# Packing routed tokens without padding: 128 two-expert tiles, and 28 one-expert boundary items run ahead of them

## The chip, the cores and the metric

The kernel runs on 1 core of one Trainium2 chip. The metric is the device time of one execution in microseconds (us); lower is better.

## What is computed

16,384 tokens of width 512 are normalised, and go through two branches whose product is added to the input. The first branch is a fixed circulant filter (computed with small matrices here) and a bit-correcting code; the second routes each token to two of eight experts:

```python
x = L0_attn_x                                   # (16, 1024, 512)
xn = _layernorm(x, axis=-1)
s = _L0_attn_ref(xn, W_el, b_el, W_le, b_le)
g = _silu(_L0_ffn_ref(xn, router_w, expert_weights))   # 8 experts of 512 x 512
x = x + s * g
...
probs = jax.nn.softmax(x @ router_w.T, axis=-1)
topk_vals, topk_idx = jax.lax.top_k(probs, 2)
topk_w = topk_vals / (topk_vals.sum(-1, keepdims=True) + 1e-06)
out = ((combined + remap_bias) * weights).sum(axis=0)  # combined: the two chosen experts' outputs
```

## The kernel before

**Stage 1** (R = 8 rounds of U = 4 groups of GT = 4 tiles of 128 tokens) loads all tokens in order, computes routing logits, and finds for each token its pair of experts. There are NQ = 28 unordered pairs. A token's number is scattered by POOL (16 indirect DMAs each round, `scatter`) into a DRAM table, `pair_tokens`, which has a region of rows for each pair. What later stages need of a token (mean, scale, two expert weights, the corrected bits) is stored as a row of 64 words in the DRAM tensor `token_info` (`weigh`, `info_store`).

**Between the stages** DVE works out from the counts of the pairs which row of `pair_tokens` each tile of stage 2 reads and which experts it uses; POOL reads these rows (`tokT`), and they are transposed into `tile_tok`, a column of token numbers for each tile. `tile_exp` holds each tile's two experts.

**Stage 2** runs over NT = 156 tiles of 128 token slots. Each pair's tokens start at a tile of their own, so a pair's last tile is partly empty; 128 tiles' worth of tokens and 27 possible partly empty tiles, rounded up to a multiple of 4, give 156. All 156 are run. Each engine goes through the tiles in an order written out by hand, and waits on semaphores for the others; a step for tile j is:

- POOL: adds the product to the input (`o2`), gathers the input rows and the `token_info` rows for tile j+4 (`gather`, two indirect DMAs), and scatters tile j's output rows (`scatter_out`).
- DVE: combines the two experts' outputs into `z2` (L970), prepares tile j+2 in `split` (sums and differences of halves, L953 to L957, then a high and a low f16 part, `hi2` L960 and `lo2` L962), copies an index for the next gather (L946), and finishes branch one (L981 to L992).
- PE: 12 matmuls of the first expert (L1133 to L1135), then `front` of tile j+1 (a bf16 transpose L1115 and eight f16 transposes L1119), 12 matmuls of the second expert, and 13 matmuls of branch one (L1147 to L1155).
- ACT: scales the first expert's output from PSUM into `t2` (L580), copies the transposes of tile j+1 from PSUM (`hl2` L573, `bT2` L574), computes silu (L586), and copies a part of branch one (L589).

The first 4 tiles and the last 4 are unrolled; those between run in a hardware loop of 4 tiles a pass.

Of the kernel before, what the change touches and what calls it, by code (L numbers as in the profile page):

```python
# [7 lines left out]
F32 = mybir.dt.float32  # L8
F16 = mybir.dt.float16
# [7 lines left out]
P = 128  # L17
# [36 lines left out]

def routing_constants(NE, cap, TB):

    pairs = [(a, b) for a in range(NE) for b in range(a + 1, NE)]
    first, second = np.asarray(pairs).T
    q = np.arange(len(pairs))
    ramp = NE - np.arange(NE)  # L60
    key = NE * (NE - first) + (NE - second)
    region = q * cap
    carry = np.tile(np.arange(TB) > 0, len(pairs))
    tile = np.arange(P)[:, None] + P * np.arange(2)[None, :]
    not_before = -(np.arange(P)[:, None] >= np.arange(P)[None, :]).astype(np.float64)
    same = np.concatenate([ramp, key, first, second, region, region // P, carry])
    return np.concatenate([np.broadcast_to(same, (P, same.size)), tile, not_before], axis=1)


def build(nc, x_in, W_el, b_el, W_le, b_le, router_w, experts, consts, out):  # L70
# [15 lines left out]
    NT = -(-(T + NQ - 1) // U) * U  # L86
# [10 lines left out]
    pair_slots = pair_tokens.rearrange("r (c o) -> (r c) o", o=1)  # L97

    ctx = ExitStack()
    with ctx:  # L100
# [3 lines left out]
        def sem(name):  # L104
# [8 lines left out]
        CW = NE + 5 * NQ + NQ * TB + 2 + P  # L113
# [26 lines left out]
        rsm = sb("rsm", [P, 26, TB])  # L140
# [11 lines left out]
        tq = sb("tq", [P, 3, NQ])  # L152
        tcmp = sb("tcmp", [P, 2, NQ + 1])
        tone = sb("tone", [P, 2, NQ])
        tmul = sb("tmul", [P, 2, NQ])
        tval = sb("tval", [P, 3, 2])
        trow = sb("trow", [P, 2], I32)
        tokT = sb("tokT", [P, 2, P], I32)
        tokTf = sb("tokTf", [P, 2, P])
        tile_tok = sb("tile_tok", [P, 2 * P], I32)  # L160
        tile_exp = sb("tile_exp", [1, 2, 2 * P], I32)
        gidx = sb("gidx", [P, U], I32)
        sidx = sb("sidx", [P, U], I32)
        small = sb("small", [P, 256])
# [11 lines left out]
        key_c, first_c, second_c, region_c, row_c = (cst[:, o + NQ * i:o + NQ * (i + 1)] for i in range(5))  # L176
        o += 5 * NQ
        carry_c = cst[:, o:o + NQ * TB]
        o += NQ * TB
        tile_c = cst[:, o:o + 2]  # L180
        nbefore_c = cst[:, o + 2:o + 2 + P]
# [28 lines left out]
        (m1, m2, mx1, mx2, zs, d2, e2, p1, p2, den, w1, w2, u1, u2, nlow, nhigh, fix, kmax, kmin, isa, isb,  # L210
         wa1, wa2, wb1, wb2, slotf) = (rsm[:, i] for i in range(26))

        oh12, ux12 = rsc[:, 2:4], rsc[:, 6:8]
        p12, w12, u12, isab, wa12 = (rsm[:, i:i + 2] for i in (7, 10, 12, 19, 21))
        far = xT4[:, :, :, :].rearrange("p b c n -> p (b c n)").bitcast(I32)[:, 0:TROWS]
        info_bits = info[:, :, 16:64].bitcast(BF16).rearrange("p t (g c) -> p t g c", g=3)
# [13 lines left out]
        bT2 = arena[0:96, 10 * E:10 * E + P].bitcast(BF16).rearrange("p (s e) -> p s e", s=2)  # L230

# [10 lines left out]
        def sems(names):  # L242
# [28 lines left out]
        rows_ready, rows_loaded, rows_float, rows_turned, exps_mm, tiles_ready = sems(  # L271
            "rows_ready rows_loaded rows_float rows_turned exps_mm tiles_ready")

        ld_x2 = [sem(f"ld_x2_{i}") for i in range(U)]
        stored = [sem(f"stored{i}") for i in range(2)]
        inf_init, gidx_ready, sidx_ready, raw_ready, uv_ready, hi_ready, split_ready = sems(
            "inf_init gidx_ready sidx_ready raw_ready uv_ready hi_ready split_ready")
        uvT_done, hl_ready, e_done, t_ready, z_ready, g_ready, y_done, y_copied, s_ready, sg_ready, o_ready = sems(
# [14 lines left out]
        def rounds(eng, count, step, head=1):  # L293
# [4 lines left out]
            with eng.Fori(head, count - 1) as i:  # L298
                for k in range(U):
                    step(i, k)  # L300
            for k in range(U):
                step(count - 1, k, last=True)

        def at(i, k, ahead):
            return i + (k + ahead) // U, (k + ahead) % U

# [878 lines left out]
```

## Time and profile before

| | |
|---|---|
| median of 3 runs | 1487.29 us (1484.12 to 1487.79) |
| span of the profiled execution, core 0 | 1491.6 us |
| PE busy | 1306.4 us, 88% |
| DVE busy | 1068.7 us, 72% |
| POOL busy | 888.9 us, 60% |
| ACT busy | 625.0 us, 42% |
| stage 1 and the preparation of stage 2 | from 0 to about 401 us |
| stage 2 | from about 401 us to the end |

The profile lists for one execution what each engine ran and when. The profiler gives no time of its own for this execution beside the span, which is 4.3 us over the median of the three timed runs. A group's idle time is the time for which its engine stood still just ahead of it. PE is TensorE's matmuls, PEld its weight loads.

### The profile page before, as it was taken

To read this page: it belongs to the slowest core of one execution; us is meant where nothing else is said; L and a number is where in the kernel's file an instruction comes from. 1 tells how busy PE (TensorE), PEld (TensorE's weight loads), DVE (VectorE), ACT (ScalarE), POOL (GpSimd) and SP (SyncE) were. 2 spreads that over 40 slices of the span, in tenths; PEclk is the share of its full clock that TensorE was granted. 3 is DMA by queue.
4 is the path that set the end of the run, shared out by engine and by line. 5 is a ranking of instruction groups with operands and counts; after the bars stand their busy time and mean duration, and the time that the engine had idled before them with its cause. 6 is when DMAs were issued, how large, how long until landed. Compare 5 with 4: busy or idle time off the path is not lost. (4 is left out here: it accounts for less than half of the span.)

```text
span 1491.6 us, 30014 instructions
## 1 busy us (share of the span) xinstructions
PE 1306.4 (88%) x8142; PEld 745.6 (50%) x8143; DVE 1068.7 (72%) x3072; ACT 625.0 (42%) x1051; POOL 888.9 (60%) x804
## 2 busy tenths in 40 slices
PE   3966776660299999999999999999999999999996
PEld 2544444330155555555555555555555555555553
DVE  7398777777177777777777777777777777777774
ACT  4654444441144444444444444444444444444442
POOL 1056565566456666666666666666666666666663
PEclk9988888785599999999999999999999999999998
DMA  9664656401112222222222212222222222222000
GB/s 348 229 211 141 155 155 155 127 15 28 36 60 84 68 73 75 74 65 72 74 71 73 79 62 71 73 74 77 67 75 62 76 69 71 77 79 63 18 0 1
DMA packets 77222, 129.97 MB, mean 87 GB/s; under 512 B 33628, under 2 KB 33746, under 8 KB 77074
## 3 DMA queue, kind: packets, MB, share of 16 engines
q0 software_dynamic: 34112, 71.58, 15.7%
q1 hardware_dynamic: 26578, 53.96, 11.2%
q10 hardware_dynamic: 16512, 4.19, 1.5%
q8 instruction: 9, 0.15, 0.0%
q14 instruction: 11, 0.09, 0.0%
HBM read 98.13 MB, written 47.12 MB: 97 GB/s over the span
## 5 line engine op out<-in xcount | busy, mean ns | idle before, releaser
L1133 PE MATMUL banks<-w_hi,arena 128*128 x1248 | 474.0, 380 | 1.4 <-issue 1.4
L1134 PE MATMUL banks<-w_lo,arena 128*128 x1248 | 474.0, 380 | 0.0
L1135 PE MATMUL banks<-w_hi,arena 128*128 x1248 | 474.0, 380 | 0.0
L970 DVE SCALAR_TENSOR_TENSOR arena<-banks,inf,arena 128x512 f32<-128x512 f32 x156 | 117.1, 751 | 259.0 <-PE banks L1135 259.0
L438 POOL TENSOR_TENSOR xbuf<-xbuf 128x512 f32<-128x512 f32 x156 | 196.5, 1260 | 162.6 <-DVE xbuf L992 162.4
L424 POOL DMA_INDIRECT xbuf<-in_L_attn_x,gidx x156 | 176.5, 1131 | 142.9 <-POOL xbuf L438 128.4
L580 ACT ACTIVATE arena<-banks,inf 128x512 f32<-128x512 f32 x156 | 121.3, 778 | 319.5 <-PE banks L1135 190.8
L573 ACT ACTIVATE arena<-banks 128x1024 f16<-128x1024 f16 x156 | 159.2, 1021 | 111.6 <-PE banks L1119 111.5
L586 ACT ACTIVATE arena<-arena 128x512 f32<-128x512 f32 x156 | 98.3, 630 | 244.9 <-DVE arena L970 244.9
L399 POOL DMA_INDIRECT pair_tokens<-tok,slot x128 | 130.6, 1020 | 114.5 <-DVE slot L877 60.9
L1135 PEld LDWEIGHTS banks<-w_hi,arena 128*128 128x128 f16 x1248 | 122.3, 98 | 146.9 <-issue 1.1
L430 POOL DMA_INDIRECT out<-xbuf,sidx x156 | 159.6, 1023 | 49.8 <-issue 48.9
L426 POOL DMA_INDIRECT inf<-token_info,gidx x156 | 157.8, 1011 | 52.5 <-issue 52.5
L1133 PEld LDWEIGHTS banks<-w_hi,arena 128*128 128x128 f16 x1248 | 122.2, 98 | 116.2 <-issue 3.1
L1134 PEld LDWEIGHTS banks<-w_lo,arena 128*128 128x128 f16 x1248 | 122.2, 98 | 112.6 <-issue 0.8
L1053 PE MATMUL banks<-xT,wcat 128*128 128x512 f32 x256 | 134.7, 675 | 32.1 <-issue 23.9
L986 DVE TENSOR_TENSOR xbuf<-xbuf 128x256 f32<-128x256 f32 x312 | 118.7, 421 | 5.4
L962 DVE SCALAR_TENSOR_TENSOR arena<-xbuf,inf,arena 128x512 f16<-128x512 f32 x156 | 117.2, 751 | 5.6
L992 DVE TENSOR_TENSOR xbuf<-xbuf,arena 128x512 f32<-128x512 f32 x156 | 108.0, 692 | 10.7
L500 ACT ACTIVATE xT<-banks 128x512 f32<-128x512 f32 x128 | 70.0, 599 | 86.8 <-remote 56.1
L1053 PEld LDWEIGHTS banks<-xT,wcat 128*128 128x128 f32 x256 | 53.5, 220 | 91.5 <-issue 82.4
L1119 PE MATMUL banks<-ident_h,arena 128*128 128x128 f16 x1248 | 96.0, 220 | 0.0
(248 smaller groups left out, 2050.0 us busy)
## 6 DMA issues: line engine op xcount, KB each, us to landing
xbuf<-in_L_attn_x SPq DMA_DIRECT2D x32, 1024.0 KB, 6.4
arena<-in_L_ffn_expert_weights SPq DMA_DIRECT2D x16, 1024.0 KB, 14.1
token_info<-info ACTq DMA_DIRECT2D x8, 512.0 KB
xbuf<-in_L_attn_x,gidx POOLq DMA_INDIRECT x156
inf<-token_info,gidx POOLq DMA_INDIRECT x156
out<-xbuf,sidx POOLq DMA_INDIRECT x156, 2.8
pair_tokens<-tok,slot POOLq DMA_INDIRECT x128
pair_tokens<-xT SPq DMA_DIRECT2D x1, 1920.0 KB, 16.2
```

The source lines that it names most:

```text
L399: pool.indirect_dma_start(out=pair_slots, out_offset=bass.IndirectOffsetOnAxis(ap=slot[:, buf, t:t + 1], axis=0), in_=tok[:, buf, t:t + 1] ...
L424: pool.indirect_dma_start(out=x2[:, k], out_offset=None, in_=x_rows, in_offset=tokens, bounds_check=N - 1, oob_is_err=False).then_inc(ld_x ...
L426: pool.indirect_dma_start(out=inf2[:, k], out_offset=None, in_=info_dram, in_offset=tokens, bounds_check=N - 1, oob_is_err=False).then_inc ...
L430: pool.indirect_dma_start(out=out_rows, out_offset=bass.IndirectOffsetOnAxis(ap=sidx[:, k:k + 1], axis=0), in_=o2[:, k % 2], in_offset=Non ...
L438: G.tensor_tensor(o2[:, b], sg2[:, b], x2[:, k], ALU.add).then_inc(o_ready, 1)
L573: nc.scalar.activation(hl2[:, b], psum[:, 0].bitcast(F16).rearrange("p (v c n) -> p v c n", v=2, c=C), ACT.Copy)
L580: nc.scalar.activation(t2[:, b], psum[:, 4 + b], ACT.Identity, scale=inf2[:, k, 3:4], bias=inf2[:, k, 2:3]).then_inc(t_ready, 1)
L986: ins = V.tensor_tensor(s2[:, b, part * H:(part + 1) * H], yp2[:, b, 0:H], ysb2[:, b, H:E], sign)
L1053: last = mm(psum[:, 2], wcat[:, c], xT4[:, k % 2, c], start=(c == 0), stop=(c == C - 1))
L1133: mm(ps, hi[:, c], wh, start=(c == 0), stop=False)
L1134: mm(ps, hi[:, c], wl, start=False, stop=False)
L1135: end = mm(ps, lo[:, c], wh, start=False, stop=(c == C - 1))
```

## The change

Tokens are now packed along a path through the 28 pairs in which neighbouring pairs share an expert (`pair_path`), without padding. A tile of 128 tokens runs with one pair of experts (head, partner). Where a pair begins inside a tile, some tokens of the tile need an expert that the tile's pair lacks; these are covered by 28 "extra" items, one for each pair: an item gathers its 128 slots, runs the one expert `PATH[n][1]`, scales the result by a coefficient that is zero for tokens that don't need it, adds it to the sum of the item before if both belong to one tile, and stores the sum (`acc2`) to DRAM (`extra_dram`). After the 28 items 128 main tiles run; each loads the sum of the item that belongs to it (`ebuf`, loaded by SP) and adds it. So the 156 steps stay 156, but 28 of them have 12 expert matmuls in place of 24 and no branch one, silu, output add or output scatter.

`token_info` now holds a weight for each of the 8 experts (columns 8 to 15), and a coefficient is picked on POOL with a mask and summed on DVE (`main_coef`). In `weigh` and `choose` some small DVE instructions fall away and two become larger. In the main tiles ACT no longer makes `t2`; DVE does, with the sum added (L1139), and ACT makes `hi2` in its place (`high_part`). DVE's `split` is cut in two: `halves_of`, now behind `t2`, and `low_part`, behind `z2`. The bias of expert outputs moves into silu.

```diff
@@ pe @@
+            def extra_step(n):
+                k, b = n % U, n % 2
+                after(pe, x_scaled, n - U + 1)
+                pe.wait_ge(hl_ready, n + 1)
+                expert(psum[:, 4 + k], b, PATH[n][1]).then_inc(x_done, 1)
+                front(*at(n // U, k, 1))
...
             front(0, 0)
-            rounds(pe, NT // U, step)
+            for n in range(NX):
+                extra_step(n)
+            main_rounds(pe, step)
@@ act @@
+            def high_part(i, k):
+                n, b = i * U + k, k % 2
+                act.wait_ge(uv_ready, n + 1)
+                after(act, uvT_done, n - 1)
+                nc.scalar.activation(hi2[:, b], uv2[:, b], ACT.Copy, scale=inf2[:, k, 1:2]).then_inc(hi_ready, 1)
+
+            def extra_step(n):
+                k, b = n % U, n % 2
+                act.wait_ge(x_done, n + 1)
+                act.wait_ge(coef_ready, n + 1)
+                after(act, acc_ready, n - 1)
+                nc.scalar.activation(t2[:, b], psum[:, 4 + k], ACT.Copy, scale=cab[:, k, 0:1]).then_inc(x_scaled, 1)
+                front(*at(n // U, k, 1))
+                high_part(*at(n // U, k, 2))
@@ act, step @@
-                act.wait_ge(e_done, 2 * j + 1)
-                after(act, z_ready, j - 1)
-                nc.scalar.activation(t2[:, b], psum[:, 4 + b], ACT.Identity, scale=inf2[:, k, 3:4],
-                                     bias=inf2[:, k, 2:3]).then_inc(t_ready, 1)
+                m, b = (i - XR) * U + k, k % 2
                 if not (last and k + 1 >= U):
                     front(*at(i, k, 1))
...
+                if not (last and k + 2 >= U):
+                    high_part(*at(i, k, 2))
@@ dve @@
+            def extra_step(n):
+                b = n % 2
+                halves_of(*at(n // U, n % U, 2))
+                dve.wait_ge(x_scaled, n + 1)
+                after(dve, extra_stored[b], 16 * (n // 2))
+                dve.wait_ge(acc_init, 1)
+                after(dve, acc_ready, n)
+                V.scalar_tensor_tensor(acc2[:, b], acc2[:, 1 - b], again[:, n:n + 1], t2[:, b], ALU.mult,
+                                       ALU.add).then_inc(acc_ready, 1)
+                gidx_copy(n // U + 1, n % U)
+                low_part(*at(n // U, n % U, 2))
+                if n + 2 >= NX:
+                    main_coef(*at(n // U, n % U, 2))
+
@@ pool @@
+            def extra_step(n):
+                if n + 2 < NX:
+                    extra_coef(n + 2)
+                else:
+                    main_coef(*at(n // U, n % U, 2))
+                pool.wait_ge(gidx_ready, n + U + 1)
+                pool.wait_ge(uvT_done, n + 1)
+                gather(n % U)
+
@@ sp @@
+            for n in range(NX):
+                sp.wait_ge(acc_ready, n + 1)
+                sp.dma_start(extra_dram[n], acc2[:, n % 2]).then_inc(extra_stored[n % 2], 16)
+            sp.wait_ge(tiles_ready, 3)
+            for b in range(2):
+                sp.wait_ge(extra_stored[b], 16 * (NX // 2))
+
+            def extra_sum(i, k, last=False):
+                m = (i - XR) * U + k
+                if not first_main(i):
+                    sp.wait_ge(t_ready, m - U + 1)
+                which = sp.value_load(tile_exp[0:1, 2, bass.ds(m, 1)], min_val=0, max_val=NX - 1)
+                sp.dma_start(ebuf[:, k], extra_dram[bass.ds(which, 1)].rearrange("o p e -> p (o e)")).then_inc(ld_e[k], 16)
+            main_rounds(sp, extra_sum)
@@ pool, main tiles @@
+            def main_coef(i, k):
+
+                m = (i - XR) * U + k
+                pool.wait_ge(ld_x2[k], 32 * (i + 1))
+                if not (first_main(i) and k < 2):
+                    pool.wait_ge(coef_sum, m - 1)
+                G.tensor_tensor(ctmp[:, k % 2], onehot[:, bass.ds(m, 1)].rearrange("p o s e -> p (o s) e"),
+                                inf2[:, k, 8:8 + NE].unsqueeze(1).broadcast_to([P, 2, NE]), ALU.mult).then_inc(coef_mul, 1)
@@ dve, weigh @@
-                V.tensor_reduce(u12, ux12.rearrange("p s n t -> p s t n"), AXX, ALU.add)
...
-                lk(V.tensor_tensor(u12, u12, w12, ALU.mult))
+                lk(V.tensor_tensor(ux12, ux12, w12.unsqueeze(2).broadcast_to([P, 2, NE, TB]), ALU.mult))
```

On PE, at the start of an extra item, the rows of the program after are these: the transposes of an item stand right ahead of its own 12 matmuls.

```order
L1312 MATMUL banks<-w_lo,arena 128x512
L1313 MATMUL banks<-w_hi,arena 128x512
L1299 MATMUL banks<-ident_b,inf 96x128 [waits hl_ready,split_ready]
L1303 MATMUL banks<-ident_h,arena 128x128 x8
L1311 MATMUL banks<-w_hi,arena 128x512 [waits hl_ready]
L1312 MATMUL banks<-w_lo,arena 128x512
L1313 MATMUL banks<-w_hi,arena 128x512
```

Before, 12 matmuls of the second expert and 13 of branch one stood between a tile's transposes and its first expert matmul; in the extra items nothing does.

On ACT, over two extra items of the program after (`cab` is the coefficient, `banks` PSUM):

```order
L682 ACTIVATE arena<-banks,cab 128x512 [waits acc_ready,coef_ready,x_done]
L668 ACTIVATE arena<-banks 128x1024 [waits x_done,uvT_done]
L669 ACTIVATE arena<-banks 96x128
L675 ACTIVATE arena<-xbuf,inf 128x512 [waits uvT_done,uv_ready]
L682 ACTIVATE arena<-banks,cab 128x512 [waits acc_ready,coef_ready,x_done]
```

The scaling of item n's output (L682) now stands ahead of the copy of item n+1's transposes (L668), for which PE waits.

On DVE, a tile of stage 2 before, from the combination of the two experts on:

```order
L970 SCALAR_TENSOR_TENSOR arena<-banks,inf,arena 128x512 [waits e_done,t_ready]
L953 TENSOR_TENSOR xbuf<-xbuf 128x256 [waits ld_x2_2]
L954 TENSOR_TENSOR xbuf<-xbuf 128x256
L956 SCALAR_TENSOR_TENSOR xbuf<-xbuf,inf 128x128 [waits raw_ready]
L957 TENSOR_TENSOR xbuf<-xbuf 128x128
L960 TENSOR_SCALAR arena<-xbuf,inf 128x512 [waits uvT_done,uv_ready]
L962 SCALAR_TENSOR_TENSOR arena<-xbuf,inf,arena 128x512 [waits hi_ready]
L946 COPY gidx<-tile_tok 128x1
L981 SCALAR_TENSOR_TENSOR xbuf<-banks,xbuf 128x128 [waits y_copied]
```

And a main tile after, at the same place:

```order
L1139 SCALAR_TENSOR_TENSOR arena<-banks,cab,arena 128x512 [waits e_done,coef_sum,ld_e1]
L1100 TENSOR_TENSOR xbuf<-xbuf 128x256 [waits hi_ready,ld_x2_3]
L1101 TENSOR_TENSOR xbuf<-xbuf 128x256
L1103 SCALAR_TENSOR_TENSOR xbuf<-xbuf,inf 128x128 [waits raw_ready]
L1104 TENSOR_TENSOR xbuf<-xbuf 128x128
L1092 COPY gidx<-tile_tok 128x1
L1150 SCALAR_TENSOR_TENSOR arena<-banks,cab,arena 128x512 [waits t_ready,e_done]
L1110 SCALAR_TENSOR_TENSOR arena<-xbuf,inf,arena 128x512 [waits uvT_done,hi_ready]
L1118 TENSOR_REDUCE cab<-ctmp 128x2 [waits x_scaled,coef_mul]
L1160 SCALAR_TENSOR_TENSOR xbuf<-banks,xbuf 128x128 [waits y_copied]
```

Two instructions are new (L1139, L1118), L960 is gone to ACT, and the sums of halves (L1100 to L1104) moved ahead of the combination (L1150).

## Rows read from the trace of the kernel before

**Rows 1.** Busy us (count) of PE, PEld, DVE, ACT, POOL; granted clock, DMA share, GB/s
```profile
700.00:800.00 100.00, 100.00 (x671) 56.58 (x669) 74.72 (x207) 42.30 (x73) 64.51 (x59) 1.00 0.23 71
```

**Rows 2.** Waits between 700 and 1400 us: total us, times, longest
```profile
DVE arena L970 <- PE banks L1135: 163.6, 102, 1.8
ACT arena L573 <- PE banks L1119: 37.3, 72, 0.6
```

**Rows 3.** Timeline of one tile on PE, and ACT's reading; start us, length us
```profile
541.80 0.38 PE L1133 MATMUL banks<-w_hi,arena 128*128 x1
...
544.17 0.38 PE L1135 MATMUL banks<-w_hi,arena 128*128 x1
...
544.39 0.22 PE L1115 MATMUL banks<-ident_b,inf 128*96 128x128 bf16 x1
...
544.44 0.61 PE L1119 MATMUL banks<-ident_h,arena 128*128 128x128 f16 x8
...
544.67 0.78 ACT L580 ACTIVATE arena<-banks,inf 128x512 f32<-128x512 f32 x1 [2.08 <-PE banks L1135]
...
544.89 0.38 PE L1133 MATMUL banks<-w_hi,arena 128*128 x1
...
547.48 0.38 PE L1147 MATMUL banks<-wle,arena 96*128 96x512 bf16 x1
...
548.69 0.38 PE L1133 MATMUL banks<-w_hi,arena 128*128 x1
```

**Rows 4.** Timeline of ACT in an unrolled tile
```profile
413.62 0.78 ACT L580 ACTIVATE arena<-banks,inf 128x512 f32<-128x512 f32 x1 [1.94 <-PE banks L1135]
414.30 1.01 ACT L573 ACTIVATE arena<-banks 128x1024 f16<-128x1024 f16 x1
```

**Rows 5.** Timeline at the first tile of stage 2, PE and ACT
```profile
398.56 1.06 PE L1119 MATMUL banks<-ident_h,arena 128*128 128x128 f16 x8
...
399.66 1.02 ACT L573 ACTIVATE arena<-banks 128x1024 f16<-128x1024 f16 x1 [55.03 <-PE banks L1119]
...
400.99 0.60 PE L1133 MATMUL banks<-w_hi,arena 128*128 x1 [1.37 <-issue]
```

**Rows 6.** Groups of ACT: busy us, mean ns, idle ahead of them
```profile
L580 ACT ACTIVATE arena<-banks,inf 128x512 f32<-128x512 f32 x156 | 121.3, 778 | 319.5 <-PE banks L1135 190.8 <-issue 128.7
...
L500 ACT ACTIVATE xT<-banks 128x512 f32<-128x512 f32 x128 | 70.0, 599 | 86.8 <-remote 56.1 <-PE banks L1044 30.7
```

**Rows 7.** Timeline of DVE in one tile
```profile
540.79 0.75 DVE L970 SCALAR_TENSOR_TENSOR arena<-banks,inf,arena 128x512 f32<-128x512 f32 x1 [1.53 <-PE banks L1135]
...
541.46 0.41 DVE L953 TENSOR_TENSOR xbuf<-xbuf 128x256 f32<-128x256 f32 x1
...
542.71 0.49 DVE L960 TENSOR_SCALAR arena<-xbuf,inf 128x512 f16<-128x512 f32 x1
...
543.23 0.75 DVE L962 SCALAR_TENSOR_TENSOR arena<-xbuf,inf,arena 128x512 f16<-128x512 f32 x1
...
543.90 0.15 DVE L946 COPY gidx<-tile_tok 128x1 int32 x1
```

**Rows 8.** Timeline from the table's reading to the first gathered data
```profile
388.94 0.29 DVE L940 CAST tokTf<-tokT 128x256 f32<-128x256 int32 x1 [21.02 <-DMA tokT<-pair_tokens,trow]
...
391.55 1.02 POOL L424 DMA_INDIRECT xbuf<-in_L_attn_x,gidx  x1 [4.00 <-DVE gidx L946]
392.88 1.00 POOL L426 DMA_INDIRECT inf<-token_info,gidx  x1 [0.31 <-issue]
...
395.78 0.42 DVE L953 TENSOR_TENSOR xbuf<-xbuf 128x256 f32<-128x256 f32 x1 [4.96 <-DMA inf<-token_info,gidx]
```

**Rows 9.** PE busy us (count), granted clock, DMA share, GB/s in two windows
```profile
401.00:407.00 6.00, 6.00 (x21) 0.50 0.18 49
...
244.00:262.00 18.00, 14.68 (x71) 1.00 0.64 210
```

**Rows 10.** The largest DVE instruction taken out of stage 1; ns min/median/max
```profile
L843 DVE TENSOR_REDUCE rsm<-rsc x8: 528/541/579, 101.6 to 350.3; 128x32 f32<-128x256 f32 x8
```

More of the change, by code:

```diff
@@ L52, in fourier_constants, with pair_path @@
     return np.concatenate([table, ka, w, np.broadcast_to(slope, (P, n))], axis=1)
+def pair_path(NE):
+    path = []
+    for head in (0, *range(NE - 1, 1, -1)):
+        path += [(head, b) for b in range(1, NE if head == 0 else head)]
+    return path
 def routing_constants(NE, cap, TB):
-    pairs = [(a, b) for a in range(NE) for b in range(a + 1, NE)]
-    first, second = np.asarray(pairs).T
-    q = np.arange(len(pairs))
+    path = pair_path(NE)
+    head, partner = np.asarray(path).T
+    low, high = np.minimum(head, partner), np.maximum(head, partner)
+    q = np.arange(len(path))
     ramp = NE - np.arange(NE)
-    key = NE * (NE - first) + (NE - second)
+    key = NE * (NE - low) + (NE - high)
     region = q * cap
[L63 to L67, printed above, removed]
+    carry = np.tile(np.arange(TB) > 0, len(path))
+    lane = np.arange(P)[:, None]
+    own = (lane == q[None, :]).astype(np.float64)
+    not_before = -(lane >= np.arange(P)[None, :]).astype(np.float64)
+    same = np.concatenate([ramp, key, head, partner, region, carry, np.arange(P)])
+    return np.concatenate([np.broadcast_to(same, (P, same.size)), lane, P * lane, own, not_before], axis=1)
 def build(nc, x_in, W_el, b_el, W_le, b_le, router_w, experts, consts, out):
@@ L302, in rounds, with main_rounds, first_main @@
                 step(count - 1, k, last=True)
+        def main_rounds(eng, step):
+            for k in range(U):
+                step(XR, k)
+            with eng.Fori(XR + 1, MR - 1) as i:
+                for k in range(U):
+                    step(i, k)
+            for k in range(U):
+                step(MR - 1, k, last=True)
+        def first_main(i):
+            return isinstance(i, int) and i == XR
         def at(i, k, ahead):
@@ L589, in step @@
+                nc.scalar.activation(g2[:, b], z2[:, b], ACT.Silu, bias=inf2[:, k, 2:3]).then_inc(g_ready, 1)
+                act.wait_ge(y_done, m + 1)
+                if not (first_main(i) and k < 2):
+                    act.wait_ge(s_ready, m - 1)
                 nc.scalar.activation(ysb2[:, b, Q:E], psum[:, 2 + b, Q:E], ACT.Copy, scale=1.0 / (XS * CS)).then_inc(y_copied, 1)
+            high_part(0, 0)
+            high_part(0, 1)
             front(0, 0)
-            rounds(act, NT // U, step)
+            for n in range(NX):
+                extra_step(n)
@@ L593, in _ @@
+            main_rounds(act, step)
         @block.vector
@@ new lines, in _ @@
+            low = 0
+            high = NE - 1
+            for head in range(NE - 1, 1, -1):
+                V.tensor_copy(before[:, high:high + head - 1], end[:, low:low + head - 1])
+                low, high = high, high + head - 1
+            V.tensor_tensor(again[:, 1:NQ], tile_of[:, 1:NQ], tile_of[:, 0:NQ - 1], ALU.is_equal)
+            V.tensor_scalar(to_tile[:, 0, 0:NX], tile_of, lane_c, None, ALU.is_equal)
+            V.tensor_scalar(to_tile[:, 1, 0:NX], tile_of, tsel[:, 1, 3:4], None, ALU.is_equal)
@@ L1120, in front, with expert @@
                 last.then_inc(uvT_done, 1)
+            def expert(ps, b, e):
+                hi, lo = hl2[:, b, 0], hl2[:, b, 1]
+                for c in range(C):
+                    wh = w_hi[:, bass.ds(e, 1), c].rearrange("p o n -> p (o n)")
+                    wl = w_lo[:, bass.ds(e, 1), c].rearrange("p o n -> p (o n)")
+                    mm(ps, hi[:, c], wh, start=(c == 0), stop=False)
+                    mm(ps, hi[:, c], wl, start=False, stop=False)
+                    end = mm(ps, lo[:, c], wh, start=False, stop=(c == C - 1))
+                return end
@@ L1143, in step @@
-                expert(1, which[1])
-                after(pe, s_ready, j - 1)
+                if first_main(i) and k < 2:
+                    pe.wait_ge(x_scaled, NX - U + k + 3)
+                else:
+                    pe.wait_ge(z_ready, m - 1)
+                expert(psum[:, 6 + b], b, which[1]).then_inc(e_done, 1)
+                if not (first_main(i) and k < 2):
+                    pe.wait_ge(s_ready, m - 1)
                 yb = psum[:, 2 + b]
```

314 lines of the change are left out of this document (194 added, 120 removed).

## The prediction

> **What bounds the kernel now.** I first read the windows of busy time. [...] A busy share of 100% can hide short stops, so I read one tile on the timeline: the first matmul of one tile starts at 541.80, that of the next at 548.69, so a tile is 6.89 us [rows 3]. Between them lie 12 matmuls of the first expert (to 544.39, 2.59 us), the transposes of the next tile (to 544.89, 0.50 us), the second expert (to 547.48, 2.59 us) and branch one (1.21 us), with nothing between. Then the list of waits: DVE stands still 163.6 us in 102 tiles, for PE [rows 2]. PE waits for nobody. Stage 2 is therefore PE's own work, 156 x 6.89 = 1075 us, and what ACT, DVE or POOL do beside it is free as long as it comes in time.
>
> **Term 1: 28 full tiles become 28 extra items.** The program still runs 156 steps. An extra item has 12 matmuls and 9 transposes: 2.59 + 0.50 = 3.09 us of PE [rows 3]. That would be the price if PE could go straight on. It can't: a tile's transposes must be copied out of PSUM by ACT before its matmuls start. In a full tile 2.59 + 1.21 us of other PE work covers that copy. In the extra items the transposes of item n+1 stand right ahead of the matmuls of item n+1, and nothing covers it. So I follow one item, counted from its first matmul:
>
> - the 12th matmul starts 2.37 us later and ends at 2.75 (544.17 and 0.38 long, against 541.80) [rows 3];
> - ACT starts on it 0.12 us later, at 2.87 (544.67 against 544.55) [rows 3]. It first scales item n's output. An activation with scale and bias from PSUM takes 0.78 us, and the next one can start 0.68 us after its start [rows 4]; a plain copy of that size takes 0.60 us [rows 6]. The new one has a scale and no bias; I take 0.60 us to the next start, so the copy of the transposes starts at 3.47. The transposes were done at 3.25 (545.05) [rows 3], so it is ACT that is late, by 0.2 us;
> - from the start of that copy to PE's next matmul it was 1.33 us at the first tile (399.66 to 400.99), in which the profile shows PE with nothing else to do [rows 5].
>
> Together 3.47 + 1.33 = 4.80 us for each item, of which PE stands still about 1.5 us. Bounds: if ACT's scaling cost nothing, 3.29 + 1.33 = 4.62 us. From above: in the hardware loop ACT starts its copy late, 37.3 us over 72 tiles or 0.52 us each [rows 2]; in the unrolled tiles it does not [rows 4], and the extra items are unrolled. With it the item is 5.35 us. I take 4.80: 28 x (6.89 - 4.80) = **-58.5 us** (-43.1 to -63.6).
>
> *Do the others keep up with 4.80 us?* DVE has, by starts, 1.25 us of halves (541.46 to 542.71), 0.67 for the low part, 0.06 for an index copy, and 0.67 for the new addition, priced as the row of L970 [rows 7]: 2.7 us. ACT has 0.6 + 1.2 + 0.5 to 0.6 for `hi2`, at most 2.5. POOL has two gathers of 1.02 and 1.00 us with 0.3 between [rows 8], some 2.6 us, and a product of one column. The longest loop goes through the gather, since only four buffers turn: end of item n's matmuls, scaling 0.8, addition and index copy 0.8, gathers and landing 4.2 (391.55 to 395.78) [rows 8], halves 1.3, high and low part 1.5, transposes 0.7, ACT's copy 1.3, matmuls 2.8, and some 0.5 of semaphores: 13.9 us, against 4 x 4.80 = 19.2 allowed. It has 5 us of room, so a slower landing is hidden.
>
> **Term 2: the start.** Stage 2 starts at the lower level of the clock: 0.50 from 401 to 407 [rows 9], so the first expert costs 5.1 in place of 2.6 us before and after. After, a stop follows it, and the second item can fall into the low level as well, for 2.6 us more. I take half, **+1.3** (0 to +2.6).
>
> **Term 3: between the stages.** DVE has more to work out (longer masks over 28 pairs, a one-hot table of 2048 columns), but it stands idle for 21.02 us before 388.94, waiting for the table [rows 8]; some 5 us more work is hidden there. On the path behind it are three small masks, two slightly larger matmuls, and `hi2` made on another engine: **+1** (0 to +2).
>
> **Term 4: stage 1.** `weigh` loses the reduction L843, 0.54 us in each of 8 rounds [rows 10], and some five small ones, and two become larger: about 0.6 to 0.9 us less each round. A bound from both sides: 0 where DVE waits anyhow, -6 where it sets the pace of a round. DVE is not the only one late there, so I take **-1**.
>
> **Term 5: from items to main tiles.** SP loads no sum before all are stored. Counted from the last item's first matmul: scaled at 3.5, added at 4.3, stored 2.9 later and loaded 2.9 after that, with the landing of a gather as the price (392.88 to 395.78) [rows 8], and 0.5 for registers: 10.6. The first main tile's first expert ends at 4.8 + 2.75 = 7.6, so DVE stands 3 us. The next tile's matmuls are prepared already. PE needs DVE again for the transposes of tile 2, at 4.8 + 6.89 + 2.59 = 14.3; DVE gets there by 10.6 + 0.7 + 1.3 + 0.1 + 0.7 + 0.7 = 14.1. It just fits. If the two transfers take 4 us more, PE waits for these: **+0.5** (0 to +4).
>
> **The 128 main tiles: 0.** PE's work in them is the same. DVE gets L1139 (priced as L970, 0.67) and a small reduction (some 0.2), and gives L960 (0.52) to ACT [rows 7]; from 75% [rows 1] it goes to about 80%. ACT loses 0.68 and gets about 0.6. POOL's 65% grows by one 16-column product, some 0.3 us or 4%. The order even helps: before, the low part ended at 543.98 and PE wanted it for the transposes at 544.39, 0.4 us of room [rows 3, 7]. After, the halves stand behind the first expert, and only the low part behind the second, so it is done 1.7 to 2 us earlier. What is wanted earlier is the gather: halves start 3.1 us sooner. By the rows the gather's chain then ends about 1 us ahead, and the first 2 us of lateness would only eat the new room. If this cover went, each 0.1 us a tile would cost 12.8 us.
>
> **Sum**: -58.5 + 1.3 + 1 - 1 + 0.5 = -56.7 us. The profiled execution's span is 1491.6, so its span after is 1435; the median of the runs is 4.3 us below the span, and I keep that distance: **1431 us**, 3.8% faster. With all low ends: -63.6 - 6 = -69.6, 1418. With all high ends: -43.1 + 2.6 + 2 + 0 + 4 = -34.5, 1453.
>
> **The rivals.**
>
> *The clock falls in the items (slower).* Place: the 28 items. PE would be busy for some 65% of each, with a stop after each burst. [...] Against it: in stage 1 PE was busy 14.7 of 18 us (with stops up to 1.3 us) and the clock stayed at 1.00 [rows 9]; but the items' stops are a little longer and come 28 times. [...] 6%.
>
> [...]
>
> *The main tiles get longer.* Place: DVE's in-order queue, with the load of the sum, the coefficient and the gather all awaited ahead of `t2`; in the hardware loop each wait also needs registers. If this adds 0.3 us a tile: 128 x 0.3 = +38, 1469. For it: DVE's share and the earlier need for the gather. Against: 2 us of room. 8%.
>
> *An item costs PE's work alone*, 3.09 us: 28 x 3.80 = -106, 1383. It would need the copy to be covered, and by the order of instructions it is not. 3%.
>
> *The gathers set the items' pace*: POOL or a landing over 5 us late. An item of 5.5 us would give 1451. Against: the 5 us of room. 5%.
>
> **Chances.** The forecast has 78%. The range 1418 to 1452 covers it and the gather's case, and leaves out 17%. What a measurement here can tell from no change is about 0.3%, 4.5 us. Slower by more: the clock's case, less its milder forms, 5%. Same: 3%. Faster: 92%.
>
> **What would show it.** In the profile after: matmul bursts of the items 4.8 us apart, with about 1.5 us of idle PE each, ended by ACT's copy; a granted clock of 1.00 from the second or third item on; main tiles 6.89 us apart; DVE idle about 3 us at the first main tile; stage 2 still starting near 401. I am wrong if the items are 3.1 or over 5.5 us apart, if the clock reads 0.50 among them, or if the main tiles are longer than 6.9 us.

## The result, and the profile after

The changed kernel is slower, not faster: 1665.18 us median of 4 runs (1658.17 to 1671.07) against 1485.7 us for the kernel before (4 runs, 1479.17 to 1487.79), a ratio of 1.1224 with a 95% interval of 1.1176 to 1.1271. The forecast was 1431 us. The first thing to look at is the page. These are the span, the busy time of the engines and the clock that TensorE was granted (one digit for each of 40 slices of the span, in tenths of full speed) of the kernel after:

```profile
span 1659.2 us, 29289 instructions
PE 1235.6 (74%) x7443; PEld 677.2 (41%) x7444; DVE 1125.9 (68%) x2981; ACT 615.5 (37%) x1023; POOL 884.1 (53%) x903
PEclk9987888857999999999999999999999999999998
```

No engine is near 100%, and the clock is up, from 0.941 to 0.948 in the mean of the profiled execution, so the engines wait for one another. The windows say in which part: busy time of PE, PEld, DVE, ACT and POOL, the granted clock, DMA share and GB/s, first over the extra items, then in the main tiles:

```profile
392.00:524.00 132.00, 92.44 (x588) 48.10 (x586) 74.07 (x194) 65.40 (x111) 61.98 (x84) 0.99 0.37 116
600.00:700.00 100.00, 80.07 (x508) 42.67 (x507) 68.50 (x170) 33.51 (x56) 54.51 (x56) 0.98 0.30 92
```

PE is at 80% in the main tiles, where it was at 100 [rows 1], and DVE and POOL are both *less* busy than before in a stretch of the same length, though each has more to do in a tile. How long is a tile? Branch one has one matmul in each, so its first and last start (the two numbers after the durations) give the pitch:

```profile
L1344 PE MATMUL banks<-wle,arena x128: 381/381/382, 530.2 to 1647.8; 96*128 96x512 bf16 x128
```

(1647.8 - 530.2) / 127 = 8.80 us, against 6.89 [rows 3]. The items are as forecast. Their first matmuls on PE, and ACT between two of them:

```profile
391.46 0.61 PE L1311 MATMUL banks<-w_hi,arena 128*128 128x512 f16 x1 [1.71 <-ACT arena L669]
...
395.25 0.38 PE L1311 MATMUL banks<-w_hi,arena 128*128 128x512 f16 x1
...
397.91 0.39 PE L1311 MATMUL banks<-w_hi,arena 128*128 128x512 f16 x1 [1.35 <-ACT arena L669]
...
439.99 0.38 PE L1311 MATMUL banks<-w_hi,arena 128*128 128x512 f16 x1 [1.44 <-ACT arena L669]
...
444.68 0.38 PE L1311 MATMUL banks<-w_hi,arena 128*128 128x512 f16 x1 [1.44 <-ACT arena L669]
```

```profile
442.77 0.69 ACT L682 ACTIVATE arena<-banks,cab 128x512 f32<-128x512 f32 x1 [2.32 <-PE banks L1313]
443.36 1.02 ACT L668 ACTIVATE arena<-banks 128x1024 f16<-128x1024 f16 x1
444.26 0.27 ACT L669 ACTIVATE arena<-banks 96x128 bf16<-96x128 bf16 x1
```

An item is 444.68 - 439.99 = 4.69 us, PE stands still 1.44 us in it, and ACT's copy ends the stop. The first takes 397.91 - 391.46 = 6.45 us: nine of its twelve matmuls are at the lower level of the clock, 0.50 from 391.46 to 395.25 (0.57 to 0.63 us each), the last three, from 395.25, and the whole second item are at 1.00 (0.38 to 0.39 us). All 28 take 133.05 us (391.46 to 524.51), so the other 27 are (524.51 - 397.91) / 27 = 4.69 us in the mean.

So the span of the profiled executions divides like this:

| stretch | before | after | difference |
|---|---|---|---|
| to the first expert of stage 2 | 401.0 | 391.5 | -9.5 |
| from there to the first branch one | 8.6 | 138.7 | +130.1 |
| first to last branch one (155 tiles, 127 tiles) | 1068.7 | 1117.6 | +48.9 |
| to the end | 13.3 | 11.4 | -1.9 |
| sum | 1491.6 | 1659.2 | +167.6 |

At 6.89 us a tile the third row would have been 127 x 6.89 - 1068.7 = -194. It is +48.9. This miss of 243 us is the surprise; the other rows together came out 18 us better than forecast, and 9.5 us of that are in the first.

Who waits for whom in the main tiles? The waits of the kernel after between 800 and 1400 us (the engine and the instruction that waited, what it waited for; total us, times, longest):

```profile
ACT arena L675 <- DVE xbuf L1104: 361.6, 68, 6.8
DVE cab L1118 <- POOL ctmp L506: 164.7, 66, 2.5
POOL xbuf L525 <- DVE xbuf L1172: 164.2, 68, 2.5
PEld banks L1299 <- DVE arena L1110: 145.1, 66, 3.7
PE banks L1299 <- DVE arena L1110: 112.5, 66, 3.2
```

The first row is ACT standing by for its next input, and it delays nobody: DVE starts the low part (L1110), which needs ACT's result, without idle time. The second and third rows name each other: DVE waits 2.5 us in each tile for POOL (164.7 / 66), and POOL waits 2.4 us in each tile for DVE (164.2 / 68). Two engines that wait for one another in the same tile are a loop of dependences, and its length is the tile. The timeline of one turn shows what is in it. First POOL, then DVE (start us, length us, idle time ahead of the row and who ended it):

```profile
1006.39 1.27 POOL L525 TENSOR_TENSOR xbuf<-xbuf 128x512 f32<-128x512 f32 x1 [2.31 <-DVE xbuf L1172]
1008.54 1.14 POOL L482 DMA_INDIRECT xbuf<-in_L_attn_x,gidx  x1 [0.87 <-POOL xbuf L525]
1009.98 1.27 POOL L484 DMA_INDIRECT inf<-token_info,gidx  x1 [0.30 <-issue]
1011.56 1.02 POOL L488 DMA_INDIRECT out<-xbuf,sidx  x1 [0.30 <-issue]
1012.61 0.22 POOL L506 TENSOR_TENSOR ctmp<-xT,inf 128x16 f32<-128x16 f32 x1
1015.34 1.26 POOL L525 TENSOR_TENSOR xbuf<-xbuf 128x512 f32<-128x512 f32 x1 [2.50 <-DVE xbuf L1172]
```

```profile
1009.61 0.75 DVE L1110 SCALAR_TENSOR_TENSOR arena<-xbuf,inf,arena 128x512 f16<-128x512 f32 x1
1012.87 0.17 DVE L1118 TENSOR_REDUCE cab<-ctmp 128x2 f32<-128x16 f32 x1 [2.50 <-POOL ctmp L506]
1013.05 0.49 DVE L1160 SCALAR_TENSOR_TENSOR xbuf<-banks,xbuf 128x128 f32<-128x128 f32 x2
1013.57 0.76 DVE L1165 TENSOR_TENSOR xbuf<-xbuf 128x256 f32<-128x256 f32 x2
1014.47 0.69 DVE L1172 TENSOR_TENSOR xbuf<-xbuf,arena 128x512 f32<-128x512 f32 x1
```

Read it round. POOL's last addition of tile m-1 (L525) starts at 1006.39. Behind it in POOL's queue stand two gathers and a scatter, so the coefficient product for two tiles on (L506, 0.22 us of work) starts only at 1012.61, 6.22 us later. DVE's reduction L1118 waits for it and starts 0.26 us later. Behind *that*, in DVE's queue, stand branch one's work and the final product L1172, for which POOL's next addition waits: it starts at 1015.34, 2.47 us on. DVE does not take branch one first: ACT has copied what L1160 reads by 1010.60, yet L1160 starts at 1013.05, behind L1118. 6.22 + 0.26 + 2.47 = 8.95 us in this turn, 8.80 in the mean. None of the rows of this loop waits for PE. PE needs 6.89 us a tile, so it waits the rest, for the low part (L1110) that DVE makes late.

### The profile page after: what moved, and what is told of

Same layout as the page of the kernel before. It is cut to its first block and busy times, and to the rows that moved or that the text cites. A ratio compares the mean times of both kernels' runs of the same rounds, so it can differ in the third digit from the quotient of the medians.

```text
span 1659.2 us, 29289 instructions
## 1 busy us (share of the span) xinstructions
PE 1235.6 (74%) x7443; PEld 677.2 (41%) x7444; DVE 1125.9 (68%) x2981; ACT 615.5 (37%) x1023; POOL 884.1 (53%) x903
## 5 line engine op out<-in xcount | busy, mean ns | idle before, releaser
L1311 PE MATMUL banks<-w_hi,arena 128*128 (+1 forms) x1136 | 433.3, 381 | 43.1 <-ACT arena L669 41.8
L1312 PE MATMUL banks<-w_lo,arena 128*128 (+1 forms) x1136 | 432.9, 381 | 0.0
L1313 PE MATMUL banks<-w_hi,arena 128*128 (+1 forms) x1136 | 432.6, 381 | 0.0
L675 ACT ACTIVATE arena<-xbuf,inf 128x512 f16<-128x512 f32 x156 | 112.5, 721 | 720.0 <-DVE xbuf L1104 720.0
L525 POOL TENSOR_TENSOR xbuf<-xbuf 128x512 f32<-128x512 f32 x128 | 162.3, 1268 | 316.4 <-DVE xbuf L1172 316.4
L1118 DVE TENSOR_REDUCE cab<-ctmp 128x2 f32<-128x16 f32 x128 | 21.7, 170 | 315.3 <-POOL ctmp L506 294.5
L484 POOL DMA_INDIRECT inf<-token_info,gidx x156 | 183.7, 1178 | 54.2 <-issue 54.2
L1299 PE MATMUL banks<-ident_b,inf 128*96 128x128 bf16 x156 | 39.1, 251 | 215.3 <-DVE arena L1110 213.4
L668 ACT ACTIVATE arena<-banks 128x1024 f16<-128x1024 f16 x156 | 159.5, 1022 | 71.6 <-PE banks L1303 71.6
L1100 DVE TENSOR_TENSOR xbuf<-xbuf 128x256 f32<-128x256 f32 x156 | 149.4, 958 | 4.9 <-DMA inf<-token_info,gidx 4.9
L488 POOL DMA_INDIRECT out<-xbuf,sidx x128 | 130.8, 1022 | 41.3 <-issue 41.3
L1110 DVE SCALAR_TENSOR_TENSOR arena<-xbuf,inf,arena 128x512 f16<-128x512 f32 x156 | 117.2, 751 | 39.2 <-ACT arena L675 25.8
L1165 DVE TENSOR_TENSOR xbuf<-xbuf 128x256 f32<-128x256 f32 x256 | 97.4, 422 | 4.4
L1139 DVE SCALAR_TENSOR_TENSOR arena<-banks,cab,arena 128x512 f32<-128x512 f32 x128 | 95.5, 746 | 4.3 <-DMA arena<-extra_sums 4.3
```

The source lines that it names most:

```text
L484: pool.indirect_dma_start(out=inf2[:, k], out_offset=None, in_=info_dram, in_offset=tokens, bounds_check=N - 1, oob_is_err=False).then_inc ...
L488: pool.indirect_dma_start(out=out_rows, out_offset=bass.IndirectOffsetOnAxis(ap=sidx[:, k:k + 1], axis=0), in_=o2[:, k % 2], in_offset=Non ...
L525: G.tensor_tensor(o2[:, b], sg2[:, b], x2[:, k], ALU.add).then_inc(o_ready, 1)
L668: nc.scalar.activation(hl2[:, b], psum[:, 0].bitcast(F16).rearrange("p (v c n) -> p v c n", v=2, c=C), ACT.Copy)
L1100: V.tensor_tensor(raw2[:, b, 0:H], x2[:, k, 0:H], x2[:, k, H:E], ALU.add).then_inc(raw_ready, 1)
L1110: V.scalar_tensor_tensor(lo2[:, b], uv2[:, b], inf2[:, k, 1:2], hi2[:, b], ALU.mult, ALU.subtract).then_inc(split_ready, 1)
```

## The experiments

The theory: this loop sets the tile, by the *place* of a small operation in two in-order queues, not by its cost. The rivals: POOL is too busy or too slow (its addition, the wider coefficient product); DVE has too much work; POOL's additions hold up DVE's; the gathers land late beside the new loads; PE loses its clock. A cut anywhere in the loop that leaves the work about as it is should bring back 6.89 us a tile under the theory, and little or nothing under the rivals.

In these experiments the kernel before ran in 1440 to 1443 us, not 1486, so each kernel is compared by its ratio to the kernel before as timed beside it on the same chip.

### e1_reduce_last: the reduction behind the final product

```
@@ DVE, step
                 if ahead:
                     low_part(*at(i, k, 2))
-                    main_coef(*at(i, k, 2))
...
                 V.tensor_tensor(sg2[:, b], s2[:, b], g2[:, b], ALU.mult).then_inc(sg_ready, 1)
+                if ahead:
+                    main_coef(*at(i, k, 2))
```

> One line moves: in a main tile DVE sums the coefficient products (the reduction L1118) as its last act of the tile, behind the final product, in place of ahead of branch one. Theory 1 (a loop through POOL: DVE waits for a product that POOL makes only after the add, both gathers and the scatter of the tile before, and the next add waits for DVE): the loop is cut, the main tiles fall from 8.75 us to PE's own 6.9 us, 128 x 1.85 = 237 us less than the changed kernel, so about 1430 us, faster than the kernel before by 3 to 4%. Theory 2 (POOL's add and DVE's two-input instructions stop each other; L1100 takes 1.05 us in place of 0.42): the instructions still overlap, so at least 128 x 0.6 = 77 us stay, above 1500 us. Theory 3 (the gathers land late beside the new loads): nothing changes, about 1665 us.

Measured: 1380.48 us (1378.76 to 1387.44), ratio 0.9587 (0.9553 to 0.9621). With the same instructions, one of 0.17 us in another place, the kernel goes from 12% slower to 4% faster. A window in the main tiles (columns as above) and branch one's matmuls:

```profile
700.00:800.00 100.00, 100.00 (x669) 56.57 (x668) 83.58 (x218) 43.89 (x73) 75.00 (x73) 1.00 0.41 120
```

```profile
L1345 PE MATMUL banks<-wle,arena x128: 380/381/383, 493.1 to 1368.3; 96*128 96x512 bf16 x128
```

PE is at 100% again and a tile is (1368.3 - 493.1) / 127 = 6.89 us. POOL at 75% and DVE at 84% are busier than in the slow kernel and PE doesn't wait for them. That rules out the amount of work on either as the cause. Additions of POOL that hold up DVE would have left the kernel above 1500 us by the expectation, and late gathers near 1665, so neither sets the tile.

### e2_product_ahead: POOL's product one tile earlier

The other cut: DVE's order stays, and POOL makes the product for three tiles on in place of two.

```
-        ctmp = sb("ctmp", [P, 2, 2, NE])
+        ctmp = sb("ctmp", [P, U, 2, NE])
...
@@ POOL, step
-                if not (last and k + 2 >= U):
-                    main_coef(*at(i, k, 2))
+                if not (last and k + 3 >= U):
+                    main_coef(*at(i, k, 3))
...
```

The lines left out adapt the buffer index and POOL's wait for a free buffer, and make the product for the third tile ahead of the first step.

> DVE's order is that of the changed kernel, the same instructions and waits at the same places. Only POOL makes each coefficient product one tile earlier (for tile m+3 at the start of its step m, with four buffers). Theory 1 (what hurts is how late the product comes, not what it costs): the product lies ready, main tiles of 6.9 us, about 1430 us. If instead the cost of the product and of the reduction in DVE's and POOL's queues is what hurts, the main tiles stay at 8.7 us and it is about 1665 us. Theory 2 (contention): at least 1500 us. A limit of theory 1: POOL now waits for the landing of the row gathered in its step before, about 1 us after its scatter; that is covered while POOL has over 0.4 us of room a tile.

Measured: 1388.69 us (1386.2 to 1393.29), ratio 0.963 (0.9606 to 0.9653). The loop is cut here too: a tile is (1379.7 - 494.1) / 127 = 6.97 us by the starts of branch one. The kernel is 0.4% behind e1. The two profiled executions are 11.3 us apart, and 10.4 of that are the 0.08 us more in each main tile. Its waits between 700 and 1200 us show a new one, since the gathered numbers are now wanted a tile earlier:

```profile
POOL ctmp L506 <- DMA inf<-token_info,gidx: 38.1, 67, 0.8
```

Whether this wait makes the longer tile was not tested.

### e3_product_on_dve: no POOL in the loop

```
...
@@ POOL, step
-                if not (last and k + 2 >= U):
-                    main_coef(*at(i, k, 2))
@@ DVE, main_coef
+                V.tensor_tensor(ctmp[:, k % 2], onehot[:, bass.ds(m, 1)].rearrange("p o s e -> p (o s) e"),
+                                inf2[:, k, 8:8 + NE].unsqueeze(1).broadcast_to([P, 2, NE]), ALU.mult).then_inc(coef_mul, 1)
                 dve.wait_ge(coef_mul, m + 1)
```

> The coefficient product of the main tiles moves from POOL to DVE, right ahead of its reduction, at the place where DVE waited. POOL is out of the coefficient altogether. Theory 1: the loop is cut, DVE has some 0.25 us more work a tile, the main tiles are PE's 6.9 us, about 1430 us. Theory 2 (contention or DVE's load): DVE gets more work, so no faster than 1600 us. Theory 3: about 1665 us.

Measured: 1380.95 us (1377.75 to 1387.71), ratio 0.9584 (0.9546 to 0.9622), the same as e1; a tile is (1370.4 - 495.1) / 127 = 6.89 us. DVE gets more work here than in the changed kernel, and the time is 15% shorter (against 1625.46 us, measured on the same chip below): DVE was not short of time.

### before_again and after_again: both kernels on one chip

No edit.

> The kernel before once more, unchanged, for its trace on the chip that the next kernels run on: the first three experiments ran on a chip on which the kernel before took 1441 us in place of 1486 us. If the chips differ in the loading of data, stage 1 is shorter here and the tiles of stage 2 are still 6.89 us; if they differ everywhere, the tiles are shorter too.

> The changed kernel once more, on the same chip as the run before it. The main tiles come to about 8.75 us and the items to 4.69 us again. If the changed kernel's stage 1 is really shorter, the first expert matmul of stage 2 again comes about 10 us earlier than in the kernel before on the same chip (391.5 against 401.0 in the first traces); if that was the chip or the run, the two come at the same time.

Measured: before 1443.5 us, after 1625.46, one run each. Against the median of six runs of before on that chip (1442.57) the ratio is 1625.46 / 1442.57 = 1.127. The main tile is again 8.80 us ((1611.9 - 494.4) / 127). The first expert of stage 2 starts at 352.19 before and 354.87 after: the set-up is 2.7 us *longer*. The other traces of this chip scatter by as much: 350.1 with the set-up of the kernel before (e5), 351.4 to 355.7 with that of the changed kernel (e1, e2, e3, e7). So no gain in the set-up shows here, and the 9.5 us by which the first two traces differ are not shown to be the change's; the runs of before differ by 9 us among themselves there.

### e5_wait_in_before: the loop built into the kernel before

If the place is all that matters, the kernel before must show the same loss once it has the same loop. It gets a product of 16 constant columns at the start of POOL's step, and on DVE a reduction of it ahead of branch one. Their result is not used.

```
...
@@ POOL, step
+                after(pool, coef_sum, j - 1)
+                G.tensor_tensor(ctmp[:, b], cst[:, 0:16], cst[:, 16:32], ALU.mult).then_inc(coef_mul, 1)
                 pool.wait_ge(sg_ready, j + 1)
@@ DVE, step, behind gidx_copy
+                dve.wait_ge(coef_mul, j + 1)
+                V.tensor_reduce(csum[:, b:b + 1], ctmp[:, b], AXX, ALU.add).then_inc(coef_sum, 1)
```

> The converse: the kernel before, with only the pattern of the coefficient added. At the start of each step POOL multiplies 16 columns of a constant, and DVE sums them ahead of branch one, waiting for POOL; nothing uses the sum. Theory 1 (the loop through POOL): the product of step j stands behind the add, gathers and scatter of step j-1, and DVE waits for it ahead of the final product of tile j, so each tile takes about 8.7 us in place of 6.9 us, 156 x 1.8 = 280 us more, a ratio of about 1.19. If instead the changed kernel lost its time by the loads of sums, the moved halves or DVE's greater load, none of which is here, this kernel stays within 1% of the kernel before.

Measured: 1710.93 us (1708.14 to 1716.01), ratio 1.1871 (1.1828 to 1.1914). A tile is (1695.4 - 357.4) / 155 = 8.63 us by the starts of branch one, where 8.7 was expected, and its waits between 700 and 1400 us have the same pair as the changed kernel:

```profile
DVE csum L982 <- POOL ctmp L440: 201.5, 80, 4.2
POOL xbuf L443 <- DVE xbuf L999: 195.1, 81, 2.5
```

(1708.7 - 1441.7) / 156 tiles = 1.71 us more in each. The two new instructions take 0.23 and 0.17 us; their place costs four times their work.

### e8_second_add: is POOL's addition a cost of its own?

In the slow tiles DVE's first instruction of the halves, L1100, takes 1.06 us where L1101, of the same shape, takes 0.41:

```profile
1006.89 1.06 DVE L1100 TENSOR_TENSOR xbuf<-xbuf 128x256 f32<-128x256 f32 x1
1007.87 0.41 DVE L1101 TENSOR_TENSOR xbuf<-xbuf 128x256 f32<-128x256 f32 x1
```

It begins while POOL's addition runs (1006.39 to 1007.66) and ends 0.29 us behind it. In the kernel before the same instruction (L953) took 0.41 to 0.48 us in all 156 tiles; here its median is 1.05. On top of e1, POOL adds once more into a spare tile:

```
+                G.tensor_tensor(spare2[:, b], sg2[:, b], x2[:, k], ALU.add)
                 G.tensor_tensor(o2[:, b], sg2[:, b], x2[:, k], ALU.add).then_inc(o_ready, 1)
```

> The first experiment's kernel with one more POOL addition of the same inputs, into a spare tile that nothing reads, ahead of each output add. Question: what does DVE's L1100 (two SBUF inputs, 0.41 us alone, 1.05 us in the changed kernel's main tiles) do while POOL adds? If POOL's additions block it for their whole length, L1100 ends with POOL's add, so the additions being two, its longest cases grow from 1.08 us towards 2.3 us. If the two only share bandwidth, it stays at 1.1 us at most. POOL's step grows from about 6.4 to 7.7 us and sets the tile: 128 x 0.8 = 100 us above the first experiment.

Measured: 1489.69 us in one run, before 1440.12 on its chip (median of 7). One of the longest cases, DVE, then POOL (L1102 and L1103 are L1100 and L1101 here; over all tiles L1102 takes 0.41 to 1.91 us, 0.75 in the median):

```profile
905.03 1.82 DVE L1102 TENSOR_TENSOR xbuf<-xbuf 128x256 f32<-128x256 f32 x1
906.77 0.41 DVE L1103 TENSOR_TENSOR xbuf<-xbuf 128x256 f32<-128x256 f32 x1
```

```profile
904.07 1.27 POOL L526 TENSOR_TENSOR arena<-xbuf 128x512 f32<-128x512 f32 x1
905.29 1.26 POOL L527 TENSOR_TENSOR xbuf<-xbuf 128x512 f32<-128x512 f32 x1
```

The DVE instruction ends at 906.85, 0.3 us behind the end of POOL's second addition, so it was held for as long as POOL added. Sharing alone would by the expectation have left it at 1.1 us at most. The blocking is real: 0.41, 1.06 and 1.82 us for one shape with none, one and two additions of POOL over it. But it does not make the tile: L1100 stands outside the part of DVE's queue that the loop passes, and in e1, at 6.89 us a tile, it still takes 0.77 us, with DVE at 84%:

```profile
1008.76 0.77 DVE L1100 TENSOR_TENSOR xbuf<-xbuf 128x256 f32<-128x256 f32 x1
```

What made e8 slower is that POOL itself becomes the bound. Its additions into the spare tile start from 501.3 to 1479.6, 7.70 us apart, and in these 128 tiles POOL waits for DVE ahead of them only 4 times. In the turn above its own work fills the time from 904.07 to 911.80: 2.48 us for the two additions, 0.87 idle, 4.03 for the gathers and the scatter with 0.30 idle between them, and 0.35 to the end of the product.

### e7_items_overlap and e9_four_in_flight: can the items be better too?

e1 leaves PE idle 1.44 us in each item. e7, on top of e1, puts the next item's transposes ahead of the present item's matmuls on PE, ACT's copy ahead of its scaling, and DVE's sum one item later; POOL's gather also waits for the item's coefficient:

```
@@ PE, extra_step
+                front(*at(n // U, k, 1))
                 after(pe, x_scaled, n - U + 1)
                 pe.wait_ge(hl_ready, n + 1)
                 expert(psum[:, 4 + k], b, PATH[n][1]).then_inc(x_done, 1)
-                front(*at(n // U, k, 1))
@@ ACT, extra_step: front and high_part ahead of the scaling
@@ DVE, extra_step: halves, low part, index copy, then the sum of item n - 1
```

> On the kernel of the first experiment (reduction last). In the 28 items PE does the transposes of item n+1 ahead of item n's matmuls, ACT copies them and makes the high part ahead of scaling item n's output, and DVE adds an item's output one item later. Theory: what an item costs above PE's 3.1 us is ACT's uncovered copy (PE idle 1.44 us before each first matmul). With the copy under the matmuls an item takes about 3.6 us, set by the loop gather, landing, halves, low part, index, in place of 4.69: 28 x 1.1 = 30 us less than the first experiment, a ratio to the kernel before of about 0.938. Rival: DVE, ACT or POOL are the limit of the items already, and the items stay at 4.7 us.

Measured: 1369.99 us (1366.82 to 1372.08), ratio 0.9506 (0.9478 to 0.9533). That is only about a third of the gain expected over e1. From the first expert matmul (351.45) to the first branch one (475.4) less the 5.68 us of the first main tile, 28 items take 118.3 us, 4.22 each, where 3.6 was expected. The waits between 380 and 440 us:

```profile
POOL xbuf L482 <- DVE gidx L1093: 19.2, 12, 3.1
PEld banks L1306 <- DVE arena L1111: 19.1, 13, 3.1
...
DVE xbuf L1101 <- DMA inf<-token_info,gidx: 11.4, 7, 2.4
```

POOL waits for the index copy, DVE for the gather that waited for it, and PE for DVE: again a small copy behind a long row of work. By this order of instructions the gather of item n+4 goes out only when that of n+2 has landed, so two can be under way at a time. e9 moves it to the front, and POOL's gathers ahead of its coefficient product:

```
@@ DVE, extra_step
+                gidx_copy(n // U + 1, n % U)
                 halves_of(*at(n // U, n % U, 2))
                 low_part(*at(n // U, n % U, 2))
-                gidx_copy(n // U + 1, n % U)
@@ POOL, extra_step: gather(n % U) ahead of extra_coef or main_coef
```

> On the kernel with overlapped items (e7), whose items took 4.2 us: there DVE and PE wait for the landing of gathers, because the gather of item n+4 is issued only after the low part of item n+2, and behind POOL's wait for item n+2's landing. Here the index copy for item n+4 stands ahead of the halves of item n+2, and POOL issues the gather ahead of that item's coefficient. Theory: four gathers are in flight, the items fall to about 3.5 us, by POOL's own 3.1 us and DVE's order, 28 x 0.7 = 20 us less than e7, a ratio to the kernel before of about 0.937. Rival: the landing itself is the limit whatever the order, or a handshake of DVE and ACT (high part, low part), and the items stay near 4.2 us, a ratio of 0.950.

Measured: 1349.39 us (1348.04 to 1351.29), ratio 0.937 (0.9346 to 0.9394). The first transpose of each item on PE:

```profile
401.06 0.26 PE L1306 MATMUL banks<-ident_b,inf 128*96 128x128 bf16 x1
...
404.45 0.26 PE L1306 MATMUL banks<-ident_b,inf 128*96 128x128 bf16 x1
...
407.85 0.26 PE L1306 MATMUL banks<-ident_b,inf 128*96 128x128 bf16 x1
```

An item is 3.40 us, near the 3.09 of PE's work alone. Which of e9's two moves did it was not separated. This is the fastest kernel of the study, 6.3% under the kernel before, with the packing and the work kept, and only the order of instructions and one wait changed.

## Why the prediction was wrong

**The step that failed** is "The 128 main tiles: 0". It costed the coefficient as "POOL's 65% grows by one 16-column product, some 0.3 us or 4%", and the reduction as "some 0.2". Both prices were right: 0.22 and 0.17 us. What was not asked is where the product stands in POOL's queue and what stands behind the reduction in DVE's. The room was counted on DVE, in busy shares, and for the gather; the way around from POOL's addition through two gathers and a scatter to the product and back through DVE's final product was never added up. It is 8.8 us, and PE needs 6.89: 128 x 1.91 = +244 us. e1, e2 and e3 cut this loop at three places and each brings the tile back; e5 makes it in the kernel before. With these the cause is shown.

**The rival "the main tiles get longer"** named DVE's in-order queue and the coefficient, but put the waiting ahead of `t2`, assumed 0.3 us a tile, and set "2 us of room" against it; its 1469 us was 196 us short too. Such room hides work that comes late. It does not shorten a loop: with the loop closed, a tile cannot take less than the 8.80 us of its turn.

**Term 1, the items**: 4.80 us forecast, 4.69 in the steady part; the stop 1.5 forecast, 1.44 measured, ended by ACT's copy, which starts at 443.36, 1.32 us ahead of PE's next matmul (1.33 forecast). The mechanism was right: 28 x (6.89 - 4.69) = -61.6, against -58.5. (The upper bound of the term has a slip: 4.80 and 0.52 are 5.32 us, not 5.35.) That an item of PE's work alone (the third rival) was out of reach held for this order of instructions; e9 shows that it was the order, 3.40 us.

**Term 2, the start**: the clock rose from 0.50 to 1.00 at 395.25, within the first item, which cost 6.45 - 4.69 = 1.76 us more than the others. Before, PE was at the lower level (0.50 [rows 9]) from 400.99 to 407.03, 6.04 us for an expert and transposes that take 3.09 at a granted clock of 1.00, 2.95 more. So the start is 1.2 us cheaper in this pair of traces, against +1.3 forecast; the second item was not at the lower level (1.00 from 397.90 to 402.60). On the chip of e1 the lower level costs about the same before and after: 2.1 us in before_again (0.50 from 352.19 to 356.40), and 2.2 in e1 (0.50 from 353.87 to 358.00), whose first item takes 360.80 - 353.87 = 6.93 us.

**Terms 3 and 4, set-up and stage 1**: 0 together in the forecast, +2.7 us on one chip (before_again, after_again), which is within the scatter of its traces.

**Term 5, items to main tiles**: DVE stands 4.31 us, not 3, for the stored and reloaded sum, and PE has no stop from it: its matmuls follow one another from 524.51 to 540.68. The longer wait was hidden; the +0.5 is 0. The 0.5 us for registers in this term's sum and the 0.5 us of semaphores in the gather's loop of term 1 were the author's estimates; no run shows either alone. The profile after has it at the first main tile:

```profile
530.04 0.75 DVE L1139 SCALAR_TENSOR_TENSOR arena<-banks,cab,arena 128x512 f32<-128x512 f32 x1 [4.31 <-DMA arena<-extra_sums]
```

**The clock**: 0.99 over the items, so the rival that it falls there did not come about. In the slow main tiles it is 0.98 to 1.00 in windows of 100 us, where it was 1.00 [rows 1], and branch one's first matmul takes 0.381 or 0.382 us in all 128, so the clock is not what lengthened them.

**The sum without the failed step**: e1 has all parts of the change and no loop. It is 1441.06 - 1380.48 = 60.6 us faster than before on its chip; the forecast of the other terms was 56.7. The items alone are 61.6 of it, with 4.69 us an item in e1 too ((487.36 - 360.80) / 27); in its trace the set-up is 1.7 us longer than in before_again and the end 1.8 us shorter, so the small terms come to nothing there. The forecast of this part was right by its main term; that its small terms (+1.8 together) did not show is within the scatter of the set-up.

## What to carry to other kernels

Work added to an in-order engine has two prices: its duration, and its place. For each new wait, follow the loop that it closes: from the producer back through everything that stands ahead of it in its queue, and from the consumer on through everything behind it, until you are back; add this up and compare it with the time of one turn, above all when every engine has spare time. When a profile after a change shows no engine full and two engines waiting for each other in every turn, try the small instruction behind the work that the other engine is waiting for, first of all.

## What the runs showed of the hardware

**POOL's addition holds up DVE.** The 128x256 DVE instruction with both inputs in `xbuf` (L953 in the kernel before, L1100 in the changed one) took 0.41 to 0.48 us in all 156 tiles before; in the tile of [rows 7] it starts at 541.46, and POOL's addition had ended at 540.69. In the turns shown in which it overlaps POOL's additions it ends 0.28 to 0.30 us after the last of them: 0.77 us long in e1 and 1.06 in the changed kernel with one of them over it, 1.82 in e8 with two. What in the chip holds it up, no run shows. In e1 the hold-up is there (0.77 us) while PE is at 100%, and in the changed kernel it is not in the loop.

**Stage 1 took longer in the first measurement, stage 2 did not.** The kernel before took 1486 us there, and 1440 to 1443 us on both chips of the experiments; on which chip the first measurement was made is not known. The first expert of stage 2 starts at 400.99 against 352.19, and the tiles after it are 6.89 us in both. Why stage 1 is shorter in the experiments stays open; no run looked into it.
